# A graph attention layer on one core: signals once per quad, near scores ahead of a group, pieces joined after six quads

## The chip, the cores and the metric

The kernel runs on one core of a Trainium2 chip. The metric is the device time of one execution in microseconds, as the median of the runs.

## The reference

A graph attention layer with 8 heads, its residual, and then a mixture of eight experts, of which each node uses two. This is its core, shortened:

```python
h = (x @ W).reshape(N, H, C)                         # N = 3125, H = 8, C = 256
a_src = einsum('nhc,hc->nh', h, att_src); a_dst = einsum('nhc,hc->nh', h, att_dst)
e = leaky_relu(a_src[src] + a_dst[dst], 0.2)         # 50,000 edges, sorted by dst
m = segment_max(e, dst, N); e = exp(e - m[dst])
denom = segment_sum(e, dst, N)
alpha = e / (denom[dst] + EPS)
out = segment_sum(h[src] * alpha[:, :, None], dst, N)
gnn = out.mean(axis=1) + bias

x = x + gnn(layernorm(x)); x = x + moe(layernorm(x)) # 8 experts of 256 x 256, the best 2
```

Because the mean over heads comes behind the sum over edges, the weights W can be multiplied in after the sum: the kernel adds up the source rows of normalized x, weighted by alpha, per node and head.

## The kernel before, in words

A start (to about 190 us) normalizes x, multiplies it into the scores of sources and targets, and sorts out where blocks of edges end. The **group phase** (to 718 us) is what the change touches. A projection by W, the routing of nodes to experts and the experts follow, to the end of the span.

The 50,000 edges, sorted by target, are 392 blocks of 128. A quad is 4 blocks (QUAD). The blocks form nine groups: seven whole ones of 48 blocks (12 quads; WHOLE is 7), then 32 and 24. A block's edges go to at most 20 neighbouring nodes. Nodes are collected in 100 homes of 32 nodes and what runs over behind them, in an accumulator on the chip with room for three homes at a time (ACC_RING).

Every engine has its own program; they meet at semaphores:

- **POOL** gathers the source rows of each block by an indirect DMA (L780) into a ring of 96 slots, two groups. From group 2 on, ahead of each quad's four gathers, it waits until `block_done` says that the quad two groups before, whose slots it refills, is multiplied.
- **PE** multiplies in `group()`. For each quad it waits for the spread alphas (`spread_ready`), for room in the accumulator (`acc_free`, at the first block and again at the third), and makes two products a block in L1078 (four PE rows a block in the trace, eight columns of heads by 20 nodes wide). Each block's last product adds 1 to `block_done` (L1156 and L1157). The first quad of a group waits for `rescaled` too.
- Between its quads PE does small steps of the **next** group's softmax (`softmax_step`), at quad counts that stand in the call: near scores (L1087, 12 products, `near_done`) behind quad 1; turning the scores (L1094) behind 3; the pieces' gathering (L1099, `pieces_done`) behind 7; the factors' return (L1104, L1105) behind 9; the alphas' turning (L1111, `alphaT_done`) behind 11. Group 7 has (1, 6, 8, 8), the last group none. Behind the last quad comes the branch to the next group, the read of a table `far` and of two words of places; a group whose blocks lie far apart would take another branch, which isn't run on these inputs.
- **DVE** does the softmax: it joins the pieces (L1837), divides, makes the hot matrix of targets (L1773), weighs (L1862 to L1870), waits for `alphaT_done`, makes spreads 0 and 1 (L1900, one per quad, a ring of 8, each waiting for `block_done` of the quad whose place it takes), rescales the accumulator's open homes (L1887, behind all blocks of the group before), makes near hots of the next group (L1617), spreads 2 to 7, the next group's scores (L1760 to L1800, behind `near_done`) and local softmax (to L1824), and spreads 8 to 11.
- **ACT** empties a home when `block_done` has reached its last block: two copies out (L1368), two clearings (L1372, L1374), the last of which gives `acc_free`.
- **SP** loads a group's near scores when `near_done` has freed their place.

## Time and profile before

| | before |
|---|---|
| median of 3 runs | 1076.33 us (1064.79 to 1094.18) |
| the profiled execution | 1063.4 us |
| its span | 1061.7 us, 16352 instructions |
| mean granted clock of TensorE | 0.802 |
| busy: PE, DVE, POOL, ACT | 734.2, 635.8, 566.9, 362.8 us |
| gathers, L780 | 392, 379.4 us of POOL busy |
| products of blocks, L1078 | 1568 rows, 313.7 us of PE busy |

The span is one execution as the profiler recorded it. The group phase is read by the turned alphas, L1111: a group's products run from its own alphas to the next group's, since those are turned behind its eleventh quad. A wait in the trace is put down to the semaphore that came last; where the profile doesn't know the releaser it says "remote". "issue" is time in which an engine waited for nothing that the profile shows.

### The profile page before, as it was taken

The numbers are of one execution on the slowest core, as the hardware profiler recorded it, in microseconds if no ns is written. First come the engines' busy times: TensorE is split into PE (matmuls) and PEld (weight loads), VectorE is DVE, ScalarE is ACT, GpSimd is POOL, SyncE is SP. The second block draws the span as 40 slices with busy tenths as digits, with TensorE's granted clock in tenths as the row PEclk, the third lists the DMA queues.
The fourth block names the chain that finished last, engine by engine and source line by source line (L and its number), as shares of the span: only waits on it lengthen the run. The fifth ranks groups of instructions, "written<-read, shape, count | busy, mean of one in ns | idle before, by whom it ended". The sixth has DMA issues, their size and how long they took to land.

```text
span 1061.7 us, 16352 instructions
## 1 busy us (share of the span) xinstructions
PE 734.2 (69%) x3876; PEld 655.2 (62%) x3877; DVE 635.8 (60%) x1829; ACT 362.8 (34%) x795; POOL 566.9 (53%) x613
## 2 busy tenths in 40 slices
PE   4765320566664765656766647779999998659995
PEld 4764220456654755546556647778888887548884
DVE  6705448564672854646646738665778778654653
ACT  4201110256454433423221112002524441737663
POOL 2172757566666667666666661013322551567686
PEclk9556555587967868877767879989999999889998
DMA  9643334477766856757455443619998865367663
GB/s 313 172 109 81 104 94 127 147 227 238 250 224 193 236 185 199 224 159 203 145 153 157 141 130 102 220 38 348 347 365 304 315 243 163 87 157 118 106 96 40
DMA packets 102473, 192.59 MB, mean 181 GB/s; under 512 B 22875, under 2 KB 61070, under 8 KB 101728
## 3 DMA queue, kind: packets, MB, share of 16 engines
q0 software_dynamic: 30176, 69.02, 27.1%
q1 hardware_dynamic: 57616, 80.31, 23.4%
q10 hardware_dynamic: 14576, 42.02, 10.1%
q8 instruction: 46, 0.75, 0.3%
q14 instruction: 59, 0.48, 0.2%
HBM read 129.20 MB, written 64.06 MB: 182 GB/s over the span
## 4 chain that ended last, share of the span: by engine, by line
DVE 29%; PE 26%; another core or an unknown queue 16%; issue 15%; DMA 6%; ACT 3%; ACTq 1%; DVEq 1%; POOL 1%; POOLq 1%; PEld 0%; SPq 0%; PEldq 0%
PE banks L1078 10%; PE banks L1226 6%; PE banks L1266 3%; PE banks L1279 3%; DVE arena L1900 3%; DMA out<-ring 2%; DMA ring<-agg_table 2%; PE banks L1087 2%; DVE banks L1505 1%; DVE ring L1526 1%; ACT banks L1372 1%; ACT arena L1368 1%; DVE stats L1564 1%; DMA ring<-in_L_gnn_W 1%
## 5 line engine op out<-in xcount | busy, mean ns | idle before, releaser
L780 POOL DMA_INDIRECT ring<-node_table,idx x392 | 379.4, 968 | 229.4 <-issue 113.9
L1078 PE MATMUL banks<-arena,ring 128*128 128x160 f32 x1568 | 313.7, 364 | 149.0 <-issue 54.7
L1078 PEld LDWEIGHTS banks<-arena,ring 128*128 128x128 f32 x1568 | 283.9, 238 | 173.1 <-issue 172.6
L1368 ACT COPY arena<-banks 128x400 f32<-128x400 f32 x200 | 88.6, 495 | 382.3 <-PE banks L1078 165.3
L1226 PE MATMUL banks<-ring 128*128 128x264 f32 x544 | 123.1, 387 | 0.0
L1226 PEld LDWEIGHTS banks<-ring 128*128 128x128 f32 x544 | 103.0, 190 | 17.4
L924 POOL DMA_INDIRECT out<-ring x56 | 89.7, 1602 | 34.0 <-DVE ring L2217 12.2
L1900 DVE TENSOR_TENSOR arena<-hot,banks 128x640 f32<-128x640 f32 x84 | 63.8, 815 | 55.7 <-remote 34.3
L1266 PEld LDWEIGHTS banks<-ring 128*128 128x128 f32 x448 | 59.7, 200 | 26.9 <-issue 19.7
L1266 PE MATMUL banks<-ring 128*128 128x128 f32 x448 | 64.0, 288 | 17.7 <-issue 16.3
L1279 PE MATMUL banks<-arena,ring 128*128 x224 | 60.9, 396 | 5.2 <-ACT ring L1422 4.4
L1226 PE MATMUL banks<-ring,arena 128*128 128x264 f32 x256 | 58.4, 387 | 0.0
L2217 DVE SCALAR_TENSOR_TENSOR ring<-banks,job_w,ring 128x256 f32<-128x256 f32 x56 | 27.1, 483 | 47.0 <-PE banks L1279 26.7
L1372 ACT COPY banks<-zeros 128x400 f32<-128x400 f32 x100 | 50.7, 507 | 9.7 <-issue 4.6
L1226 PEld LDWEIGHTS banks<-ring,arena 128*128 128x128 f32 x256 | 48.5, 190 | 8.2
L1374 ACT COPY banks<-zeros 128x400 f32<-128x400 f32 x100 | 50.0, 500 | 0.0
L910 POOL DMA_INDIRECT slot_table<-arena,slots x42 | 42.1, 1002 | 12.7 <-issue 11.3
L1388 ACT COPY ring<-ring 128x448 f32<-128x448 f32 x30 | 29.0, 1013 | 52.3 <-DMA ring<-agg_table 37.1
L906 POOL COPY arena<-tags 128x3 f32<-128x3 f32 x21 | 3.9, 188 | 80.3 <-DVEq L2073 79.3
L1279 PEld LDWEIGHTS banks<-arena,ring 128*128 128x128 f32 x224 | 39.7, 198 | 10.2 <-issue 6.6
L1422 ACT ACTIVATE ring<-banks,b_sb 128x128 f32<-128x128 f32 x112 | 35.1, 364 | 16.6 <-issue 13.7
L891 POOL TENSOR_TENSOR ring<-ring,bias_bc 128x256 f32<-128x256 f32 x25 | 19.0, 791 | 35.7 <-DMA ring<-in_x 35.7
(421 smaller groups left out, 1022.9 us busy)
## 6 DMA issues: line engine op xcount, KB each, us to landing
agg_table<-arena ACTq DMA_DIRECT2D x100, 400.0 KB
ring<-agg_table SPq DMA_DIRECT2D x25, 1600.0 KB
ring<-slot_table SPq DMA_DIRECT2D x56, 130.0 KB
ring<-node_table,idx POOLq DMA_INDIRECT x392
near_hot<-dst_table SPq DMA_DIRECT2D x28, 192.0 KB
ring<-in_x SPq DMA_DIRECT2D x8, 640.0 KB, 11.8
ring<-in_L_gnn_W SPq DMA_DIRECT2D x4, 1024.0 KB, 9.2
arena<-in_L_ffn_w SPq DMA_DIRECT2D x16, 256.0 KB
```

The source lines that it names most:

```text
L780: pool.indirect_dma_start(rows[:, slot_of(b), :], None, node_table, bass.IndirectOffsetOnAxis(idx[:, b:b + 1], 0)).then_inc(got[got_of(g)] ...
L910: pool.indirect_dma_start(slot_table, bass.IndirectOffsetOnAxis(slots[:, k, t:t + 1], 0), tn[t % TN_RING], None).then_inc(sent[t % TN_RING ...
L924: pool.indirect_dma_start(out, bass.IndirectOffsetOnAxis(xs[j % XS_RING][:, D:D + 1].bitcast(I32), 0), ybuf[j % Y_RING], None, bounds_chec ...
L1078: m = pe.matmul(columns[:, k, bass.ds(at * (UNIT * H), SPREAD * H)], lhs[:, k * P:(k + 1) * P], weights, start=False, stop=True, skip_grou ...
L1226: m = pe.matmul(bank[proj_bank(t)][:, 0:CN], aggt[t % AGG_RING][:, k * H + h, :], W_sb[:, k, h, :], start=(k == 0 and h == 0), stop=(k == ...
L1266: m = pe.matmul(h_bank[j % 2][:, f * P:(f + 1) * P], w1_now[j % 2][:, k, f * P:(f + 1) * P], xsT[j % 2][:, k, :], start=(k == 0), stop=(k ...
L1279: m = pe.matmul(y_bank[j % 2][:, 0:D], h_sb[j % 2][:, f, :], w2_sb[:, bass.ds(e, 1), f, :].rearrange("p e n -> p (e n)"), start=(f == 0), ...
L1368: act.copy(stage[j][:, k * SLOTS * H:(k + 1) * SLOTS * H], views[k]).then_inc(drained, 1)
L1372: act.copy(views[0], zeros[:, 0:1].to_broadcast([P, SLOTS * H]))
L1374: act.copy(views[1], zeros[:, 0:1].to_broadcast([P, SLOTS * H])).then_inc(acc_free, 1)
L1422: g = act.activation(h_sb[j % 2][:, f, :], h_bank[j % 2][:, f * P:(f + 1) * P], ACT.Gelu, bias=b1_sb[:, bass.ds(e, 1), f:f + 1].rearrange( ...
L1900: dve.tensor_tensor(spread[:, s:s + QUAD, :].rearrange("p s (d h) -> p s d h", h=H), hot[:, q * QUAD:(q + 1) * QUAD, :].unsqueeze(3).to_br ...
```

## The change

PE's signal per block becomes one per quad: the quad's last product adds 4 to `block_done`. The near scores of the next group are made at the head of a group's code, ahead of the table's read and the branch, which is behind the last product of the group before; on DVE the near hots that they need move from behind the rescale to behind the weighing, ahead of the wait for the alphas. And pieces are gathered after quad 6 instead of 7.

```diff
-            def group(g, quad, slot, ring, size, nxt, steps, near_at=1, ahead_of_far=0):
+            def group(g, quad, slot, ring, size, nxt, steps, near_ahead=True, ahead_of_far=0):
                 def softmax_step(done):
-                    if turn and done == near_at:
-                        near_scores(g + 1, quad + size // QUAD, kb_of(nxt), chunks_of(nxt))
                     if done == turn:
                         turn_scores(g + 1, kb_of(nxt))
...
+                if near_ahead:
+                    near_scores(g + 1, quad + size // QUAD, kb_of(nxt), chunks_of(nxt))
                 is_far = pe.value_load(far[0:1, bass.ds(g, 1)], min_val=0, max_val=2 * NS)
...
-                            add_block(at, rows[:, (slot + q * QUAD + s) % ROOM, :], spread[:, (ring + q) % SPREAD_RING * QUAD + s, :])\
-                                .then_inc(block_done, 1)
+                            m = add_block(at, rows[:, (slot + q * QUAD + s) % ROOM, :], spread[:, (ring + q) % SPREAD_RING * QUAD + s, :])
+                        m.then_inc(block_done, QUAD)
                         softmax_step(q + 1)
...
-                    group(2 * pair + j, pair * (2 * per_group) + j * per_group, slot_of(j * GB), j * per_group % SPREAD_RING, GB, 0, (3, 7, 9, 11), ahead_of_far=7)
+                    group(2 * pair + j, pair * (2 * per_group) + j * per_group, slot_of(j * GB), j * per_group % SPREAD_RING, GB, 0, (3, 6, 9, 11), ahead_of_far=6)
...
-                      steps_of.get(g, (3, 7, 9, 11)), near_at.get(g, 1), ahead_of_far.get(g, 7))
+                      steps_of.get(g, (3, 6, 9, 11)), g < WHOLE, ahead_of_far.get(g, 6))
...
                 weigh(g)
+                if g < GROUPS - 3:
+                    near_hots(g + 1)
                 dve.wait_ge(alphaT_done, g + 1)
...
                     rescale(g, *bounds[g])
-                    if g < GROUPS - 3:
-                        near_hots(g + 1)
                     spreads(g, 2, SPREAD_RING)
```

PE's program at the head of the loop over groups, here behind the alphas' turning of the first group. The ISA rows of L1087 load the weights of its products; `near_hot` is what near scores multiply by. Before:

```order
L1111 MATMUL banks<-ident,arena 128x16x8 x2
L1200 UNCONDITIONAL_BRANCH
L1200 ISA
L1132 TENSOR_LOAD far
L1132 ISA x2
L1133 COMPARE_AND_BRANCH
...
L1147 REGISTER_ALU [waits rescaled]
L1150 REGISTER_ALU [waits spread_ready]
...
L1083 REGISTER_ALU
L1087 ISA [waits near_hot_ready]
L1087 MATMUL banks<-arena,near_hot 128x32
```

And of the change:

```order
L1111 MATMUL banks<-ident,arena 128x16x8 x2
L1200 UNCONDITIONAL_BRANCH
L1200 ISA
L1087 ISA [waits near_hot_ready]
L1087 MATMUL banks<-arena,near_hot 128x32
...
L1132 TENSOR_LOAD far
L1132 ISA x2
L1133 COMPARE_AND_BRANCH
...
L1147 REGISTER_ALU [waits rescaled]
L1150 REGISTER_ALU [waits spread_ready]
```

The twelve products of L1087 stood behind the first quad's eight and now stand ahead of the table's read; the wait for `near_hot_ready` stands ahead of the wait for `rescaled`.

DVE's program at the boundary between the first group and the second, from the last step of the weighing on; `banks` at L1887 is the accumulator. Before:

```order
L1870 TENSOR_TENSOR arena<-banks,arena 128x384 [waits dve_chain]
L1900 TENSOR_TENSOR arena<-hot,banks 128x640 [waits block_done,alphaT_done]
L1891 COPY arena<-banks 128x384
L1900 TENSOR_TENSOR arena<-hot,banks 128x640 [waits block_done]
L1883 REGISTER_ALU [waits block_done]
L1887 ISA [waits acc_free]
...
L1617 TENSOR_TENSOR near_hot<-near_hot,near_key 128x1536 [waits dve_chain,in_near]
L1900 TENSOR_TENSOR arena<-hot,banks 128x640 [waits block_done] x6
```

And of the change, where lines stand one lower:

```order
L1869 TENSOR_TENSOR arena<-banks,arena 128x384 [waits dve_chain]
L1616 TENSOR_TENSOR near_hot<-near_hot,near_key 128x1536 [waits in_near]
L1899 TENSOR_TENSOR arena<-hot,banks 128x640 [waits block_done,alphaT_done]
L1890 COPY arena<-banks 128x384
L1899 TENSOR_TENSOR arena<-hot,banks 128x640 [waits block_done]
L1882 REGISTER_ALU [waits block_done]
L1886 ISA [waits acc_free]
...
L1899 TENSOR_TENSOR arena<-hot,banks 128x640 [waits dve_chain,block_done]
L1899 TENSOR_TENSOR arena<-hot,banks 128x640 [waits block_done] x5
```

The near hots moved past two spreads, the rescale and their waits for `alphaT_done` and `block_done`; what they wait for themselves (`in_near`, the load) is as before.

## Rows read from the trace of the kernel before

**Rows 1.** The page's first line: span of the profiled execution, instructions.

```profile
span 1061.7 us, 16352 instructions
```

**Rows 2.** Windows: start:end, us, busy of PE, PEld, DVE, ACT, POOL (instructions); clock, DMA, GB/s.

```profile
190.80:264.70 73.90, 48.89 (x212) 43.22 (x213) 39.63 (x86) 36.81 (x86) 44.53 (x47) 0.68 0.66 209
...
399.80:470.10 70.30, 43.65 (x230) 39.01 (x229) 39.39 (x87) 24.76 (x58) 48.03 (x49) 0.78 0.63 197
...
612.20:665.40 53.20, 34.03 (x220) 32.49 (x221) 30.11 (x78) 8.77 (x21) 20.69 (x22) 0.84 0.38 114
```

**Rows 3.** The gathers' line, 204 to 646 us; what ended POOL's idle time before them.

```profile
L780 POOL DMA_INDIRECT ring<-node_table,idx x296: 940/946/2258, 204.5 to 642.7; - x148
...
  issue: 77.7, 255
  PE banks L1078: 40.9, 22
  remote: 38.7, 19
```

**Rows 4.** Timeline, POOL: start us, us, engine, line, operation [idle before <-releaser].

```profile
396.56 0.94 POOL L780 DMA_INDIRECT ring<-node_table,idx  x1 [2.02 <-PE banks L1078]
...
408.35 0.95 POOL L780 DMA_INDIRECT ring<-node_table,idx  x1 [2.10 <-remote]
```

**Rows 5.** Timeline around a late signal, group 2, columns as in rows 4.

```profile
370.82 0.26 DVE L1820 TENSOR_TENSOR piece_in<-chunk_sel,ends 128x96 f32<-128x96 f32 x1
...
375.21 0.33 PE L1099 MATMUL banks<-piece_in,head_sel 128*8 128x96 f32 x2
...
384.64 0.25 DVE L1837 COPY piece_all<-banks 8x96 f32<-8x96 f32 x1 [9.25 <-remote]
384.83 0.89 ACT L1368 COPY arena<-banks 128x400 f32<-128x400 f32 x2 [4.74 <-remote]
384.83 0.94 POOL L780 DMA_INDIRECT ring<-node_table,idx  x1 [1.80 <-remote]
```

**Rows 6.** Timeline: scores at the start, and near scores of group 4.

```profile
59.66 9.53 PE L1002 MATMUL banks<-va,ring 128*128 128x8 f32 x44
...
88.77 0.37 DVE L1544 TENSOR_TENSOR score_all<-banks,rstd 128x200 f32<-128x200 f32 x1 [40.00 <-remote]
...
416.30 3.01 PE L1087 MATMUL banks<-arena,near_hot 128*128 x24
...
426.01 0.56 DVE L1798 TENSOR_TENSOR edge_e<-ring,banks 128x384 f32<-128x384 f32 x1 [4.88 <-remote]
```

**Rows 7.** Timeline: the boundary from group 2 to group 3.

```profile
399.75 0.49 PE L1111 MATMUL banks<-ident,arena 128*128 128x128 f32 x3
...
408.16 0.82 DVE L1900 TENSOR_TENSOR arena<-hot,banks 128x640 f32<-128x640 f32 x1 [8.71 <-remote]
...
411.72 1.76 DVE L1617 TENSOR_TENSOR near_hot<-near_hot,near_key 128x1536 f32<-128x1536 int32 x1 [0.51 <-DVE banks L1887]
...
411.88 4.63 PE L1078 MATMUL banks<-arena,ring 128*128 128x160 f32 x16 [8.81 <-DVEq L1888]
```

**Rows 8.** Waits, 190 to 705 us: line <- releaser: us in total, times, longest.

```profile
PE banks L1078 <- ACT banks L1374: 42.2, 17, 5.9
...
DVE piece_all L1837 <- remote: 32.9, 5, 9.2
...
DVE piece_all L1837 <- issue: 7.8, 1, 7.8
...
DVE edge_e L1798 <- remote: 6.1, 2, 4.9
...
DVE edge_e L1798 <- PE banks L1087: 5.2, 2, 3.4
```

**Rows 9.** Timeline: ACT drains one home.

```profile
378.39 0.89 ACT L1368 COPY arena<-banks 128x400 f32<-128x400 f32 x2 [4.69 <-PE banks L1078]
...
379.58 0.51 ACT L1374 COPY banks<-zeros 128x400 f32<-128x400 f32 x1
```

More of the change, by code:

```diff
@@ L1155, in group @@
                                 skip_runtime_bounds_check_because="a byte of places is 32 * (home % 3) + less than 16")
-                            add_block(at, rows[:, (slot + q * QUAD + s) % ROOM, :], spread[:, (ring + q) % SPREAD_RING * QUAD + s, :])\
-                                .then_inc(block_done, 1)
+                            m = add_block(at, rows[:, (slot + q * QUAD + s) % ROOM, :], spread[:, (ring + q) % SPREAD_RING * QUAD + s, :])
+                        m.then_inc(block_done, QUAD)
                         softmax_step(q + 1)
                 with pe.Else():
-                    far_steps = sorted({n for n in (*steps, near_at) if turn and n})
+                    far_steps = sorted({n for n in steps if turn})
                     for done in far_steps:
@@ L1201, in _ @@
                 for j in range(2):
-                    group(2 * pair + j, pair * (2 * per_group) + j * per_group, slot_of(j * GB), j * per_group % SPREAD_RING, GB, 0, (3, 7, 9, 11), ahead_of_far=7)
+                    group(2 * pair + j, pair * (2 * per_group) + j * per_group, slot_of(j * GB), j * per_group % SPREAD_RING, GB, 0, (3, 6, 9, 11), ahead_of_far=6)
             steps_of = {WHOLE: (1, 6, 8, 8), GROUPS - 1: (0, 0, 0, 0)}
-            near_at = {WHOLE: None}
             ahead_of_far = {WHOLE: 1, GROUPS - 1: 0}
```

## The prediction

> **What bounds the kernel now.** The span is 1061.7 us [rows 1]; the profiled execution took 1063.4 us, 12.9 below the runs' median of 1076.33, so a sum made on the profile is moved up by 12.9 for the median. The change touches the group phase alone, and I read first which engine paces it, by the engines' busy time in single groups. From one group's turned alphas to the next's take 73.90 us in the first group and 70.30 in the fourth; PE is busy 48.89 and 43.65 of that, DVE 39.63 and 39.39, POOL 44.53 and 48.03 [rows 2]. No engine is full. Group 6, during which the gathers end, takes 53.20 us for the same 48 blocks.
>
> So the next view is the line that issues the gathers. From 204.5 to 642.7 us it issues 296: 438.2 / 296 = 1.48 us each, 71 per 48 [rows 3]. Without a stop one costs 0.946 us and 77.7 / 255 = 0.305 us to issue: 1.25, or 60.0 per 48. The rest is 40.9 + 38.7 = 79.6 us in 41 stops, in all of which POOL waits for a quad of two groups before ("remote" is a wait whose releaser the profile doesn't name; it ends by the same signal) [rows 3]. Two such stops stand 11.79 us apart, 396.56 to 408.35 [rows 4], and that is eight gathers (8 x 1.25 = 10.0) and a stop of about 1.8. Six of these are 70.7 us, a group's time. **POOL's cycle of eight gathers and one wait for PE's signal is the period**, and 41 x 0.305 of the stops would be issue anyway: 79.6 - 12.5 = 67 us, or 1.64 a stop, is all that earlier signals can give while gathers last.
>
> Why does the signal come so late? In the timeline PE gathers the pieces at 375.21 and is done within 0.33 us; DVE takes them at 384.64 after 9.25 us of idleness, and ACT and POOL, which wait for other things, are released at 384.83, 0.2 us later [rows 5]. PE's signals thus arrive in bursts, and the burst falls where POOL stands and its transfers run dry. There are two readings: late because there are many signals, one per block, or late because the products queued ahead of them are done later than their records say. For the first speaks that the small steps with a single signal are late only behind blocks. Against it speaks the start of the program: 44 products of the score line end at 59.66 + 9.53 = 69.19 with one signal, and DVE, which stands 40.00 us for it, is released at 88.77, 19.6 us later, with no block signal yet sent [rows 6]. I go by the second at about three to one.
>
> **The change, part by part.** (a) *392 signals become 98.* Every quad's last product still signals, and POOL waits for whole quads, so no gather can be released by an earlier block than before. By the second reading the saving is 0. By the first, lateness shrinks up to fourfold; the bounds are 0 and the 67 us of POOL's stops. I take 0, the nearer to the start's one late signal.
>
> Here the Trainium skill speaks for a gain: "TensorE: Matmul & The Clock Gate", section "The cost: per-tile semaphore tail", gives each increment about 26.3 ns of serial tail and calls a single one on the last product sound. By it, as an estimate, 294 increments fewer would be 7.7 us of PE. No row here shows that tail.
>
> (b) *Near scores before the first quad.* Before, PE makes them behind the first quad: in group 3 at 416.30, 3.01 us of products, and DVE takes them at 426.01 after 4.88 us of waiting [rows 6]. Now they stand behind the last quad of the group before. There PE stands 8.81 us anyway until the first product of group 3 at 411.88, because DVE, though the alphas were turned at 399.75 + 0.49 = 400.24, got them at 408.16 and rescales first [rows 7]. The 3.0 us fit in it with 5.8 to spare, where the table read and the branch, which come behind them now, have to lie too. Without that cover they would cost the 3.0 us that they take, 21 in the seven groups in which they are moved. On DVE the 1.76 us of near hots [rows 7] move from behind the rescale to ahead of the alphas' wait, which lasts 8.71 us [rows 7]: hidden. Where DVE has no such wait, the same 1.76 us are before the first spreads instead of behind them, and PE's first quad is later by that. The wait for near scores (6.1 + 5.2 = 11.3 us in four waits [rows 8]) goes: about 11.3 / 6 = 2, with the 1.76 some 3 us a group off the softmax chain on DVE.
>
> (c) *Pieces joined a quad sooner.* DVE stood for the pieces 32.9 + 7.8 = 40.7 us in six waits [rows 8]. A quad is 70.7 / 12 = 5.9 us, so the join moves up by at most 5.9 where DVE's input to it is ready. It nearly is: in group 2 DVE had it at 370.82 + 0.26 = 371.08, 4.1 us before PE came to it [rows 5], and (b) makes it 3 earlier, 7.1 against the 5.9 needed. Where it isn't ready, PE would stand, with its products and so POOL's signal behind it, for the remainder, at most the 5.9. What is late next is the burst: the join ends when PE's signal arrives, and this moves in whole cycles of POOL.
>
> (b) and (c) together make the chain from flags to alphas up to 9 us shorter per group. But the chain isn't what paces a group: POOL is. How much of the 9 us reaches POOL no row says: 0 if its cycle doesn't notice, 6 x 9 = 54 if all of it does. I choose one stop less per group, 6 x 1.64 = 10 us, near the lower end, since POOL's stops in the middle of a group, as at 396.56 [rows 4], lie far from what the chain delivers. Behind the last gather the chain does count: there a quad is 53.20 / 12 = 4.4 us [rows 2], and with the 1.76 of near hots that is 6 us, once (group 7 keeps its steps).
>
> (d) *ACT drains later.* ACT waited for the block with which a home ends; now it hears of the quad's last. Of the 100 homes only 24 end on a quad's last block (counted from the sorted edges), so 76 are handed over one to three blocks later. A drain takes 378.39 to 380.09, 1.70 us [rows 9], and three homes of room lie ahead of PE. PE stood for ACT's clearing 42.2 us in 17 waits [rows 8]. With bursts as above, a block's own signal came with its quad's anyway, so I take 0. Without that cover it is up to three blocks, 3 x 5.9 / 4 = 4.4 us, per wait.
>
> Sum: 0 - 10 - 6 + 0 = -16. From 1063.4 that is 1047; on the runs' median 1076.3 - 16 = **1060 us**, 1.5% faster.
>
> **The rivals.**
> *The signals were the delay.* For: the bursts release three engines at once [rows 5]. Against: the start [rows 6]. POOL's stops then shrink to half or to their floor, -34 to -67, and with the tail's 6: 1036 to 1003; I put it at 1015, chance 0.19.
>
> *The chain paces more than I think.* Where DVE stands 8 to 9 us for pieces and alphas at a boundary [rows 5, 7], spreads come late and PE with them; the change would then give PE some quads of lead, half the 54 and the tail: -30, 1046. Chance 0.13.
>
> *A signal costs PE's own time.* Four blocks' 16 product records take 4.63 us with their four signals [rows 7], 1.16 us a block; if a tenth of that were the signal's, 294 fewer would be 34 us of PE. PE bounds only once the gathers are over, with some 80 blocks left (32 and 24 of the last two groups, and the end of group 6's 48): 60 signals fewer, 7 us, 1076.3 - 16 - 7 = 1053. Against it: PE stands idle a third of every group [rows 2], so elsewhere it wins nothing. Chance 0.03. The Trainium skill's tail (same page and section) is the rule for this rival.
>
> *ACT's drains come late and PE stands for them.* This is the case that ends slower. In groups 0 and 1 some 21 homes end per group (counted from the edges), 1.75 a quad, each 1.70 us of ACT [rows 9], so ACT's work for a quad is 3.0 of its 5.9 us. If the quad's first home, which it could start some two blocks sooner, now begins with the second, PE's first products of the next quads wait for room. At 1 us a quad over the 24 quads of these two groups that is +24: 1100. It decides from about 0.7 us a quad on (24 x 0.7 = 17 eats the 16). For it: the 42.2 us that PE already stands there [rows 8]. Against it: the lateness of every signal. Chance 0.17.
>
> *Nothing comes of it.* POOL's cycle doesn't notice, the tail is off the end: 1076, within the "same" below.
>
> **How the numbers follow.** Forecast and "nothing" together 0.48: 0.30 for about 1060, 0.18 for about 1076. Signals 0.19, chain 0.13, a signal's own cost 0.03, ACT 0.17. The runs of before lie between 1064.79 and 1094.18, so about 2% (1055 to 1098 as limits) is what a measurement can tell from no change. Faster by more: signals, chain and the signal's own cost, 0.35. Slower: 0.17. The range goes from 1014, which leaves out the signals' far half (0.09), to 1097, which leaves out most of ACT's case (0.10). The likeliest case's own range is 1045 to 1076: the 10 us of stops may be 0 or 20, and the tail 0 to 6.
>
> **What would show it.** (a) right: POOL's stops still near 1.6 us beyond issue, 30 to 41 of them between the same gathers, and DVE's release after the start's scores as late as 88.8; wrong: most stops gone, gathers at 1.3 us each. (b): near scores end before the first quad, and DVE's wait for them is gone; wrong if PE's idle time at the boundary grows beyond 8.8 us. (c): pieces on DVE a cycle earlier and no PE wait for its input above 2 us. (d): PE's wait for ACT's clearing stays near 42 us; at 60 and more the slower rival holds. A time below 1040 makes the reading of the lateness wrong, one above 1090 that of ACT or of the boundary.

## The result, and the profile after

In the first measurement the changed kernel took 1089.66 us (median of 4 runs, 1084.04 to 1102.49) and before took 1077.28 (4 runs, 1064.79 to 1094.18). The ratio of these medians is 1.0115; the ratio on record is 1.0226, 95% interval 1.0181 to 1.0272: slower, where 1.5% faster was forecast, though the interval doesn't settle whether by more than 2%. The runs of both kernels fall into clusters, and the ratio on record leaves out what lies over 1.5% above a kernel's fastest run and so hangs on where that one run fell (for e1 below it gives 1.0118, 1.0051 to 1.0186, where the medians over all runs stand at 0.998), so that below I give medians and differences of means over all runs instead (one run of before of 3647.81 us apart).

The profiled execution of the changed kernel is a late one, 39.1 us longer than that of before [rows 1]. The page's first line and its row of the products (busy us, mean ns | idle before, what ended most of it):

```profile
span 1100.8 us, 16330 instructions
...
L1078 PE MATMUL banks<-arena,ring 128*128 128x160 f32 x1568 | 313.7, 366 | 128.6 <-ACT banks L1373 70.1
```

PE is busy with blocks as long as before, 313.7 us. The times of L1111 in the timeline tell where the 39 us are. The first group's alphas are turned at 229.85 us, in before at 190.84 (190.80 is where the first stretch of [rows 2] begins): 39 us late already. Group 7's are turned at 703.8 and 665.4: still 38 us. **The whole difference of these two profiles lies ahead of the groups**, in a stretch whose code the change does not touch. The timeline of the changed kernel there (start us, us, engine, line, operation [idle before <-releaser]):

```profile
146.16 5.16 PE L1087 MATMUL banks<-arena,near_hot 128*128 128x32 f32 x24
...
202.07 0.55 DVE L1797 TENSOR_TENSOR edge_e<-ring,banks 128x384 f32<-128x384 f32 x1 [35.47 <-remote]
...
229.85 0.90 PE L1111 MATMUL banks<-ident,arena 128*128 128x128 f32 x3 [5.18 <-DVE arena L1869]
...
231.65 5.32 PE L1087 MATMUL banks<-arena,near_hot 128*128 x24 [0.90 <-DVE near_hot L1616]
...
236.78 5.26 PE L1078 MATMUL banks<-arena,ring 128*128 128x160 f32 x24
...
241.23 0.94 POOL L780 DMA_INDIRECT ring<-node_table,idx  x1 [43.13 <-PE banks L1078]
```

And of before:

```profile
149.65 5.16 PE L1087 MATMUL banks<-arena,near_hot 128*128 128x32 f32 x24
...
153.58 0.94 POOL L780 DMA_INDIRECT ring<-node_table,idx  x1 [7.55 <-issue]
...
157.62 0.56 DVE L1798 TENSOR_TENSOR edge_e<-ring,banks 128x384 f32<-128x384 f32 x1
```

The near scores of group 0 were made by 146.16 + 5.16 = 151.3 us, and DVE took them at 202.07, 50.7 us later, when POOL had made its last gather of the first two groups (197.2). In before the same products ended at 154.8, behind a stop of POOL of 7.55 us, and DVE took them at 157.62 without having waited; the changed kernel's POOL stopped there too, but for 4.40 us alone (to 153.07). Everything behind hangs on the 97th gather, the first that needs a quad finished: 241.23 here, 204.52 in before, and the span ends 860 and 857 us behind it.

The groups themselves, with what answers to [rows 2], [rows 3] and [rows 8]. Windows (start:end, us, busy of PE, PEld, DVE, ACT, POOL; clock, DMA, GB/s), groups 0, 3 and 6:

```profile
229.85:301.30 71.45, 48.45 (x212) 44.34 (x213) 40.96 (x87) 34.75 (x80) 39.24 (x40) 0.69 0.64 203
434.50:508.30 73.80, 46.19 (x230) 42.54 (x229) 40.07 (x87) 26.11 (x60) 47.77 (x50) 0.75 0.60 181
647.20:703.80 56.60, 42.21 (x222) 38.18 (x221) 29.88 (x78) 10.31 (x24) 22.41 (x24) 0.76 0.36 112
```

The gathers' line, and what ended POOL's idle time before them:

```profile
L780 POOL DMA_INDIRECT ring<-node_table,idx x296: 940/946/2422, 241.2 to 679.8; - x148
...
  issue: 79.3, 260
  PE banks L1078: 73.7, 14
  remote: 41.4, 22
```

296 gathers in 679.8 - 241.2 = 438.6 us, in before in 438.2 [rows 3]. Without the one stop of 43.13 POOL stands 72.0 us in 35 stops; before, without its first of 4.47, 75.1 in 40. **POOL's stops, and with them the time of the groups together, are what they were in these two profiles.** The waits (line <- releaser: us in total, times, longest) show that inside the group much has moved all the same:

```profile
PE banks L1078 <- ACT banks L1373: 70.1, 24, 6.2
...
DVE edge_e L1797 <- remote: 38.3, 3, 35.5
...
PE banks L1078 <- DVEq L1887: 9.7, 4, 6.2
...
DVE piece_all L1836 <- remote: 3.8, 3, 1.3
```

and of before the row that [rows 8] leaves out:

```profile
PE banks L1078 <- DVEq L1888: 45.9, 6, 13.5
```

DVE's wait for the pieces fell from 40.7 us to 6, and PE's wait for DVE's rescale at the boundaries from 45.9 to 9.7. PE's wait for ACT's clearing rose from 42.2 to 70.1. At the boundary into group 3, the place of [rows 7], the near scores stand where the idle 8.81 us were:

```profile
434.51 0.49 PE L1111 MATMUL banks<-ident,arena 128*128 128x128 f32 x3
...
438.39 0.82 DVE L1899 TENSOR_TENSOR arena<-hot,banks 128x640 f32<-128x640 f32 x1 [5.83 <-remote]
...
440.37 4.63 PE L1078 MATMUL banks<-arena,ring 128*128 128x160 f32 x16 [5.37 <-ACT banks L1373]
...
444.80 2.94 PE L1087 MATMUL banks<-arena,near_hot 128*128 x24
...
448.44 0.74 PE L1078 MATMUL banks<-arena,ring 128*128 128x160 f32 x2 [0.70 <-issue]
```

The boundary costs PE 0.70 us now, as the change meant, but 8 us earlier it stood 5.37 for ACT.

### The profile page after: what moved, and what is told of

Read it like the earlier page. It is cut to its first block, busy times and chain, and to the rows that moved or that the text cites. A ratio compares the mean times of both kernels' runs of the same rounds, so it can differ in the third digit from the quotient of the medians.

```text
span 1100.8 us, 16330 instructions
## 1 busy us (share of the span) xinstructions
PE 747.9 (68%) x3876; PEld 673.0 (61%) x3877; DVE 635.2 (58%) x1829; ACT 363.6 (33%) x795; POOL 563.2 (51%) x613
## 4 chain that ended last, share of the span: by engine, by line
PE 29%; DVE 20%; issue 16%; another core or an unknown queue 15%; DMA 7%; ACT 4%; POOL 3%; ACTq 2%; POOLq 2%; DVEq 1%; PEld 0%; SPq 0%; PEldq 0%
PE banks L1225 10%; PE banks L1078 8%; DMA out<-ring 5%; PE banks L1002 4%; DVE arena L1899 3%; POOL ring L780 2%; ACT banks L1371 2%; ACT arena L1367 1%; PE banks L1265 1%; PE banks L1278 1%; DVE banks L1504 1%; PE banks L1050 1%; DMA ring<-in_x 1%; ACTq L1353 1%
## 5 line engine op out<-in xcount | busy, mean ns | idle before, releaser
L780 POOL DMA_INDIRECT ring<-node_table,idx x392 | 379.4, 968 | 263.0 <-issue 112.4
L1078 PE MATMUL banks<-arena,ring 128*128 128x160 f32 x1568 | 313.7, 366 | 128.6 <-ACT banks L1373 70.1
L1078 PEld LDWEIGHTS banks<-arena,ring 128*128 128x128 f32 x1568 | 288.3, 241 | 149.7 <-issue 149.0
L1371 ACT COPY banks<-zeros 128x400 f32<-128x400 f32 x100 | 50.7, 507 | 8.5 <-issue 4.5
L1002 PE MATMUL banks<-va,ring 128*128 128x16 f32 (+1 forms) x200 | 40.4, 341 | 17.6 <-issue 17.3
L1002 PEld LDWEIGHTS banks<-va,ring 128*128 128x128 f32 x200 | 41.8, 314 | 16.6 <-issue 16.2
L910 POOL DMA_INDIRECT slot_table<-arena,slots x42 | 41.5, 987 | 12.7 <-issue 11.3
L1278 PEld LDWEIGHTS banks<-arena,ring 128*128 128x128 f32 x224 | 40.1, 200 | 10.8 <-issue 7.1
## 6 DMA issues: line engine op xcount, KB each, us to landing
ring<-in_x SPq DMA_DIRECT2D x8, 640.0 KB, 12.1
```

The lines of the kernel that those rows point to most:

```text
L780: pool.indirect_dma_start(rows[:, slot_of(b), :], None, node_table, bass.IndirectOffsetOnAxis(idx[:, b:b + 1], 0)).then_inc(got[got_of(g)] ...
L910: pool.indirect_dma_start(slot_table, bass.IndirectOffsetOnAxis(slots[:, k, t:t + 1], 0), tn[t % TN_RING], None).then_inc(sent[t % TN_RING ...
L1002: m = pe.matmul(bank[score_bank(a, t)][:, t * n:(t + 1) * n], xT[:, t, k * P:(k + 1) * P], va[:, k, 0:H + NX] if a == 0 else va_of[1][:, k ...
L1078: m = pe.matmul(columns[:, k, bass.ds(at * (UNIT * H), SPREAD * H)], lhs[:, k * P:(k + 1) * P], weights, start=False, stop=True, skip_grou ...
L1278: m = pe.matmul(y_bank[j % 2][:, 0:D], h_sb[j % 2][:, f, :], w2_sb[:, bass.ds(e, 1), f, :].rearrange("p e n -> p (e n)"), start=(f == 0), ...
L1371: act.copy(views[0], zeros[:, 0:1].to_broadcast([P, SLOTS * H]))
```

## The experiments

**Theories.** S: the loss is ahead of the groups, where PE's signals wait behind gathers for a time that varies, and the change has little part in it. A: one signal per quad makes ACT drain later. N: near scores and pieces stand in the wrong place.

Each series ran before beside its kernels, on one chip. The table has every run that gave a time: medians in us, and the difference of the means to before of the same series with its 95% half-width (1.96 standard errors, which is too narrow for rows of 4 to 6 runs: the first row's would be 18.6 by Student's t). "Early start" and "held" are explained below.

| kernel | runs | median | before, runs | difference |
|---|---|---|---|---|
| the change, first measurement | 4 | 1089.7 | 1077.3, 4 | +13.1 +- 14.5 |
| e1, the change again | 12 | 1080.2 | 1082.7, 23 | +1.3 +- 7.4 |
| e2, the change, signals per block | 6 | 1079.1 | same | +0.4 +- 9.2 |
| e3, before, signals per quad | 6 | 1080.3 | same | +0.2 +- 10.5 |
| e4, before, near scores ahead | 12 | 1071.9 | same | -4.0 +- 7.6 |
| e5, before, held | 12 | 1072.2 | 1075.5, 35 | -5.1 +- 4.2 |
| e6, the change, held | 12 | 1075.2 | same | -1.7 +- 4.0 |
| e7, as e6, groups 0 and 2 behind | 12 | 1074.6 | same | -3.6 +- 3.4 |
| e8, as e6, signals per block | 12 | 1072.9 | same | -4.4 +- 3.3 |
| e9, the change a third time | 6 | 1082.2 | 1080.0, 17 | -2.6 +- 8.8 |
| e10, before, narrow gathers | 8 | 1078.9 | same | -3.7 +- 8.0 |
| e11, before, early start | 6 | 1060.8 | same | -18.6 +- 7.1 |
| e12, the change, early start | 12 | 1071.2 | 1078.4, 23 | -6.5 +- 6.1 |
| e13, before, early start | 12 | 1062.3 | same | -13.9 +- 5.7 |
| e14, as e12, groups 0 and 2 behind | 12 | 1067.7 | 1079.8, 24 | -11.7 +- 5.0 |
| e15, as e12, signals per block | 6 | 1063.6 | same | -11.9 +- 8.4 |
| e16, the change, early start | 12 | 1066.4 | same | -12.1 +- 5.2 |
| e17, before, early start | 6 | 1061.1 | same | -16.9 +- 5.6 |
| e18, before, early start, signals per quad | 12 | 1067.4 | 1079.5, 17 | -15.6 +- 4.9 |

### The change again, and its parts alone (e1 to e4, e9)

e1 and e9 are the changed kernel itself. e2 undoes its first part, e3 makes that part alone, and e4 the second part alone:

```diff
-                            add_block(...).then_inc(block_done, 1)
+                            m = add_block(...)
+                        m.then_inc(block_done, QUAD)
```

> The changed kernel itself, once more, for a second profile. In its first profile the whole difference to before lies ahead of the groups: first alphas turned at 229.85 us instead of 190.84, because the near scores' signal of group 0 reached DVE 50 us late, and from there to the turned alphas of group 7 it took 473.9 us against 474.5. Theory S (the start): the start is late by a varying amount from run to run, so this profile has first alphas somewhere between 190 and 230 us and 474 us of groups behind it. Theory A (ACT): the drains start later, so PE's wait for ACT's clearing is again at 60 us or more (70 in the first profile, 42 before), and the groups take longer than 474 us wherever the start is on time, by about 20 us. Theory N: the loss is in the order of near scores and pieces, and this shows as PE standing at the boundaries.

> The change without its first part: a signal per block again, near scores ahead and pieces after six quads. Theory A: PE's wait for ACT falls back to about 42 us and the time to the kernel's before or below it, 1060 to 1077. Theory S: as slow as the change where the start is late, whatever the signals; the time lies with the change at about 1088. Theory N: as slow as the change, with the loss at the boundaries.

> The kernel before with the first part alone: one signal of 4 per quad. Theory A: slower than before by about the whole 2%, 1088 to 1100, and PE's wait for ACT at 60 us and more. Theory S: no difference to before except through the start, 1065 to 1090 with the groups at 474 us. Theory N: as before, 1077. If the number of signals were what makes them late, this one would be faster than before by 30 us or more.

> The kernel before with the second part alone: near scores ahead of a group's first quad, near hots ahead of the wait for the alphas. Theory N: slower than before by most of the 2%, 1085 to 1095, with PE's first products of a group later behind the turned alphas than the 11.6 us of before. Theory A: as before or up to 10 us faster, 1066 to 1077. Theory S: no difference other than by the start.

> The changed kernel a third time, beside more runs of before, to see how much of the 2.26% is a matter of which runs were drawn. Theory S: both kernels have the same two or three clusters of times, set by how late the near scores' signal of group 0 is, and the change adds some 4 us ahead of the first product: medians within 1% of each other, the ratio between 0.995 and 1.012. Theory A or N, a steady cost in the groups: again 1.015 to 1.025.

e1's profile is as late as the first one: near scores made by 146.0, their signal at 202.1, the 97th gather at 241.0, the end 859 us behind it. e9's is on time: 150.5, 151.4, 206.2, and 860. In e2 the signal was 18.6 us late and the 97th gather at 222.4. Over all profiles of this study the 97th gather goes between 199.8 and 241.2 us, and the end is 854 to 873 us behind it, with no order by kernel. The three series together have 22 runs of the changed kernel and 44 of before: medians 1082.6 and 1080.8, difference of the means +2.2 +- 5.4 us. The 2.26% of the first four runs did not come back. e3 and e4 lie under what A and N had wanted of them (1088 to 1100 and 1085 to 1095), and e3 isn't the 30 us faster that it would be if the number of signals made them late. Beyond that the parts alone can't be told from before in these runs: the spread of one kernel, some 40 us, hides whatever they do. That speaks for S and says how much has to be taken out before A and N can be judged.

### The start held (e5 to e8)

One wait more on POOL, ahead of the last 36 gathers of group 1, in before (e5) and in the changed kernel (e6). e7 makes near scores of groups 0 and 2 behind the first quad again (and group 0's near hots behind the rescale), e8 signals per block.

```diff
             first_far_scores()
+            pool.wait_ge(near_done, 1)
             gather(1, AHEAD_OF_TABLES, GB)
```

> The kernel before, with one wait added on POOL: ahead of the last 36 gathers of group 1 it waits until DVE could take the near scores of group 0, so that this signal no longer stands behind gathers. Theory S (the start decides): in six profiles so far the first refilling gather (the 97th) went between 204.5 and 241.2 us and the span ended 857 to 865 us behind it, whatever the kernel; the signal came 0 to 56 us late. With the wait it comes within 5 us, the 97th goes at 203 to 210 us in every run, and the times gather at 1060 to 1070 us, without the 1077 to 1093 us that 18 of 23 runs of before showed. If the lateness is not from gathers, the spread of the runs stays, and the wait costs 5 to 50 us.

> The changed kernel with the same wait on POOL. Theory S: the spread goes here too, and what is left against the other kernel with the wait is the change's own effect. From the profiles: near scores ahead of the first group cost 4 us there (6.0 us from the turned alphas to the first product instead of 2.3), from the 97th gather to the last is 2 to 4 us shorter (434 to 436 against 438), the tail behind it 1 to 3 us longer: within 5 us of the other kernel, 1064 to 1072. Theory A (ACT's drains): 15 to 25 us slower than the other kernel with the wait.

> As the changed kernel with the wait on POOL, but near scores in groups 0 and 2 are made behind the first quad, and group 0's near hots behind the rescale, as before the change. If the 4 us ahead of group 0's first product are what the change loses where the start is on time, this is 3 to 6 us faster than the one with all near scores ahead, and first products come 2 to 3 us behind the turned alphas. If not, the same.

> The changed kernel with the wait on POOL, and a signal per block again. Theory A, that one signal per quad makes ACT late: faster than with one per quad by 5 to 20 us, and PE's wait for ACT falls from 60 or more to about 42 us. Theory S: the same within 4 us; signals neither cost nor bring anything, since POOL's cycle of eight gathers holds the groups.

The timeline of e5 shows what a gather does to the signal and what the end of the gathers does:

```profile
135.73 5.17 PE L1088 MATMUL banks<-arena,near_hot 128*128 128x32 f32 x24
...
148.16 0.95 POOL L780 DMA_INDIRECT ring<-node_table,idx  x1 [0.30 <-issue]
...
153.04 0.56 DVE L1799 TENSOR_TENSOR edge_e<-ring,banks 128x384 f32<-128x384 f32 x1 [8.45 <-remote]
153.17 0.94 POOL L780 DMA_INDIRECT ring<-node_table,idx  x1 [4.07 <-remote]
```

The scores were made by 140.9, the signal came 4 us after POOL's last gather was issued, at 149.1, to DVE and POOL at once. The spread went from 37 us (before, 35 runs, 1066.62 to 1103.74) to 18 in e5, 13 in e6 and 9 in e7 and e8, and none of these 48 runs is above 1084.1; of before 8 of 35 are. So S holds for the upper part of the spread; the median of before fell by 3 us only, and the expected 1060 to 1070 was too low. The change is 3.4 +- 3.9 us slower than the other held kernel, e8 0.7 +- 3.2, e7 1.5 +- 3.3: small, and not placed.

### What holds the gathers (e10)

```diff
-                    pool.indirect_dma_start(rows[:, slot_of(b), :], None, node_table,
+                    to, table = (rows[:, slot_of(b), :], node_table) if g < 2 else (rows[:, slot_of(b), 0:H], score_table)
+                    pool.indirect_dma_start(to, None, table,
```

> The kernel before, where from group 2 on each gather brings 8 numbers a row (32 bytes) from the table of scores instead of 264; the other columns keep what the ring held, so the sums are of old rows. As many gathers, as many rows, the same waits, 1/33 of the bytes. What it tells: why PE's signals come late and what paces a group. If it is the bytes in flight, signals come within 1 us, POOL's stops go, and a group takes POOL's 60 us or less. If it is the number of rows or POOL's issuing, the stops and the 71 us per 48 gathers stay as they are.

```profile
L781 POOL DMA_INDIRECT ring<-score_table,idx x295: 940/947/2284, 204.2 to 642.1; - x148
...
  issue: 77.1, 253
  remote: 40.8, 23
  PE banks L1079: 36.4, 19
```

The same stops, 77.2 us in 42, the same 438 us, with 1/33 of the bytes. (The trace has 295 of the 296 gathers; the start of this kernel gathers whole rows as before.) So it isn't the volume of data that makes PE's signals late in the groups or a group 71 us long; what is left is the gathers' number, their 128 rows each, or their issuing, and no run here tells these apart.

### The second scores first (e11 to e13, e16, e17)

At the start DVE waits for a signal that stands alone [rows 6]. POOL now makes 8 gathers and then waits for that signal itself (with e5's wait further on):

```diff
-            gather(0, 0, AHEAD_OF_VECTORS)
-            pool.wait_ge(va_summed, 2)
-            gather(0, AHEAD_OF_VECTORS, AHEAD_OF_STRETCHES)
+            gather(0, 0, 8)
+            pool.wait_ge(score_done, 3)
+            gather(0, 8, 17)
...
```

> The kernel before with POOL's start put otherwise: after 8 gathers it waits for the second scores' signal of PE, then makes 9 more, the stretches and the rest, and ahead of the last 36 gathers of group 1 it waits for the near scores' signal. If PE's signals are late behind gathers, also one that stands alone, DVE takes the second scores at 70 to 74 us instead of 88.8, the first alphas are turned 10 to 16 us sooner, at 175 to 182, and the time falls by 5 to 14 us, to where POOL's own 96 gathers allow. If the lateness at the start has another cause, DVE takes them near 88 and POOL's wait costs what it lasts, 10 us or more.

> The changed kernel with the start put as in e11_start_scores_first, beside that kernel. With the early start PE is ready for its first product some 15 us before POOL has finished its first 96 gathers, so the 4 to 11 us that near scores ahead of group 0 cost are hidden there. Theory S: nothing is left of the change: within 4 us of the other, both near 1060. Theory A or N, a steady cost in the groups: 8 us and more slower than the other.

> The kernel of e11_start_scores_first once more, as what the changed one with the same start is held against on the same chip: 1056 to 1065 us, and 1.0 to 2.0% faster than before.

> The changed kernel with the early start again (the kernel of e12_change_scores_first), beside the two that undo a part and the one that undoes all: 5 to 9 us slower than the one that undoes all.

> The kernel before with the early start again (that of e13_before_scores_first), against which the other three are held: 1056 to 1065 us in the median.

Timeline of e11:

```profile
47.18 21.50 PE L1003 MATMUL banks<-va,ring 128*128 128x8 f32 x100 [0.27 <-DVE va L1539]
...
68.72 0.36 DVE L1545 TENSOR_TENSOR score_all<-banks,rstd 128x200 f32<-128x200 f32 x1 [20.47 <-PE banks L1003]
...
68.95 0.94 POOL L780 DMA_INDIRECT ring<-node_table,idx  x1 [10.46 <-PE banks L1003]
```

The products end at 47.18 + 21.50 = 68.68, as in before at 69.19 [rows 6]. Without gathers behind them DVE has the signal 0.04 us later, with them it had it 19.6 us later. **That shows the cause of the lateness: gathers in flight, and one signal is enough to be late.** Over the three series the kernel before with this start takes 1061.9 us (median of 24 runs, none above 1074.5) against 1079.1 for before without it (143 runs of all series, 29% of them above 1085): 16.5 +- 2.6 us faster in the mean, the best version of this study. That is the worth of both waits together, since e11 has e5's too.

With most of the start's variation gone the change can be judged: 24 runs each, 1067.9 against 1061.9, difference of the means **+6.1 +- 3.1 us, 0.6%** (+7.4 +- 4.6 in e12 and e13, +4.8 +- 4.3 in e16 and e17). S, which wanted nothing left, falls for this part; the 8 us and more of A or N are above the mean, though inside its interval. The start isn't pinned altogether: in e13's profile the near scores' signal came before POOL had to wait for it, the gathers went on without a stop to 194.2, and the first alphas were turned at 205.65, where the other six profiles of e11 to e17 have 178.5 to 182.3.

### Which part costs the 6 us (e14, e15, e18)

e14 is the changed kernel with the early start and the near scores of groups 0 and 2 behind the first quad (and group 0's near hots behind the rescale), e15 that with signals per block, e18 before with the early start and signals per quad alone.

> The changed kernel with the early start, but near scores of groups 0 and 2 behind the first quad and group 0's near hots behind the rescale. On one chip the changed kernel with the early start was 7.4 us (plus or minus 4.6) slower than before with it, and its first product came 13.2 us behind the turned alphas against 2.1. If these 11 us ahead of the first product are the cost, this kernel is 4 to 9 us faster than the changed one with the early start, and its first product is 2 to 3 us behind the alphas. If the cost is in the groups behind, the same within 3.

> The changed kernel with the early start and a signal per block again. If one signal per quad costs (ACT hears of a home's end up to three blocks late; PE's wait for ACT 62 to 71 us instead of 41 to 53), this is 4 to 9 us faster than the changed one with the early start. If PE's wait for ACT only takes the place of other waits, the same within 3.

> The kernel before with the early start and the first part of the change alone, one signal of 4 per quad. Over three chips the early start took 1061.9 us (median of 24 runs) without the change and 1067.9 (24 runs) with it. If one signal per quad costs these 6 us (ACT's drains later, PE's wait for ACT at 60 us and more), this kernel lies at 1066 to 1070, 1.0% under before. If not, at 1060 to 1064, 1.6% under before, and the cost is in the order of near scores or pieces.

The first group in e12, where gathers are in flight when its alphas are turned:

```profile
180.55 0.90 PE L1112 MATMUL banks<-ident,arena 128*128 128x128 f32 x3 [6.55 <-DVE arena L1870]
...
182.25 5.32 PE L1088 MATMUL banks<-arena,near_hot 128*128 x24 [0.80 <-issue]
...
194.70 0.89 PE L1079 MATMUL banks<-arena,ring 128*128 128x160 f32 x2 [7.13 <-remote]
...
205.34 0.94 POOL L780 DMA_INDIRECT ring<-node_table,idx  x1 [7.42 <-PE banks L1079]
```

and in e14:

```profile
179.85 0.90 PE L1112 MATMUL banks<-ident,arena 128*128 128x128 f32 x3 [4.95 <-DVE arena L1872]
182.83 2.50 PE L1079 MATMUL banks<-arena,ring 128*128 128x160 f32 x8 [2.08 <-issue]
```

Near scores ahead put 13.2 us between the turned alphas (181.45) and the first product; behind, 2.1. But in e14 the 97th gather goes at 203.3, only 2 us sooner than in e12, and the kernel is only 1.6 +- 3.3 us faster than the changed one (e12 and e16 together; against e16 of its own series it is 0.4 +- 3.5 slower). Most of the 11 us are hidden behind POOL, which is not done with its first 96 gathers before 197.

For the signals, PE's wait for ACT in e16 (signals per quad) and in e17 (per block):

```profile
PE banks L1079 <- ACT banks L1374: 60.8, 19, 5.9
```

```profile
PE banks L1079 <- ACT banks L1375: 51.9, 19, 5.8
```

Over the ten profiles with signals per block it is 40.0 to 52.8 us, mean 46.6, over the ten with one per quad 52.1 to 75.1, mean 64.2. The two groups differ in more than the signal, and the order of near scores matters: with near scores ahead the wait goes from a mean of 45.4 us (e2, e4, e8, e15) to 66.5 (the eight profiles of the change, e7 and e14 among them), with them behind the first quad as in before from 47.5 (six profiles) to 55.0 (e3 and e18). So the signal per quad makes PE stand longer for ACT, some 8 us by itself and some 21 together with near scores ahead.

What of it reaches the end isn't settled. e18 is 4.1 +- 3.2 us slower than before with the early start in the other series, but as far under the before of its own series (-15.6) as those were under theirs (-13.9 to -18.6), and its profile makes the second scores 7 us later than those of e12 to e17, ahead of anything that was changed; e15 has four runs at 1059 to 1064 and two at 1078 to 1079, and tells nothing. Nor do the profiles show a loss in the groups: from the 97th gather to the end of the span it is 859.5 us in the mean of six profiles with the groups of before (before, e5, e10, e11, e13, e17) and 859.4 in six of the change (the first, e1, e6, e9, e12, e16), a difference of -0.1 +- 5.0. **Where the 6 us are lost stays open.** The Trainium skill's tail of 26.3 ns an increment ("TensorE: Matmul & The Clock Gate", "The cost: per-tile semaphore tail") would spare PE in e18, as an estimate, 7.7 us; no run here shows such a gain, and 4.1 +- 3.2 points the other way.

## Why the prediction was wrong

**The forecast's sign** was wrong: 16 us faster stood against 13.1 slower in the first four runs; over all runs without an added wait it is +2.2 +- 5.4, with the start held +3.4 +- 3.9, with the early start +6.1 +- 3.1. No set of runs shows the gain; "nothing comes of it", chance 0.18, is nearest. Two steps failed: the gain of (b) and (c), 16 us of which none was measured, and the start, a term that was put at nothing.

**(b) and (c) together** is where the 16 us were lost: "I choose one stop less per group, 6 x 1.64 = 10 us" measured 1.6 us in the first profile: 72.0 us in 35 stops less 35 x 0.305 is 61.3, before 75.1 in 40 gives 62.9. Over the six profiles of each named above the 296 gathers take 437.3 us with the change and 438.1 without, 0.9 +- 2.1 less. The shorter chain did reach PE, 36 us less standing at the boundaries, but PE then stood 28 us longer for ACT, and POOL's gathers took as long as before. The 6 us behind the last gather didn't come either: from it to the last product it is 75.0 us in before and 76.3 in the changed kernel, 77.4 and 77.9 over the six of each.

**What I did not price at all** is the start. I took the profiled span of before, 12.9 us under its median, as the kernel's own time, and moved the sum up by 12.9 as if that were the same in both kernels. But the start varies from run to run: the 97th gather went 37 us later in the first profile of the change than in that of before, and with POOL waiting for two signals before fell to a median of 1061.9, with none of 24 runs above 1074.5. Late signals behind gathers are the largest varying term that the profiles show, up to 56 us for the near scores of group 0. Since the first difference did not come back in e1 and e9, most of it was this and not the change; four runs of each were too few, and +13.1 +- 14.5 holds zero.

**What bounds the kernel.** That POOL's gathers and its stops pace the groups held in every profile (eight gathers are the commonest stretch between two stops, 22 of 38 in before; 4 and 12 occur as well). That the number of signals is not what makes them late was right: with 98 signals instead of 392 POOL stands as long [rows 3 and the row of L780 above], and the start, which I had taken for the deciding row [rows 6], decided it when tried (e11).

**(a)** 0 was right for the lateness.

**(b)** The step "the 3.0 us fit in it with 5.8 to spare" held at the boundary into group 3 and failed at the first group, for which I had not read the row: there PE has no such idle time, and the first product moved from 2.1 to 6.0 us behind the turned alphas, or to 13 where gathers were in flight. DVE's waits went as said: the one for the pieces from 40.7 to 6 us, that for near scores inside the groups from 11.3 to 2.8 (38.3 without the first of 35.5).

**(d)** "I take 0" may be the step that had the sign, but that is argued and not shown. PE's wait for ACT rose by 28 us in the first profile, over the 60 that I had named for the slower rival, while that rival's +24 is far above the 6 us that were seen in all. "With bursts as above, a block's own signal came with its quad's anyway" is therefore false for part of the homes. The wait took the place of others in good part: the groups of the profiles are no longer for it.

**The range** of 1014 to 1097 holds 1089.66, but mostly because it was wide for the other side. One rival's sum is off: half the 54 and the tail's 6 are 33, not 30, so that it should have stood at 1043.

## What to carry to other kernels

When runs of one kernel spread by more than the effect looked for, find first what the spread is in the trace and pin it; here one wait of POOL for another engine cut it from 37 to 18 us, and with a second one further ahead before ran 16 us faster. A shorter chain is worth what the pacing engine loses by it, so price it there, and ask of each signal made rarer which waiter wanted the early one. A step that idle time covers at one boundary has to be looked up at the first one too, where there may be none.

## What the runs showed of the hardware

Signals. A signal of PE that stands alone came 0.04 us after its products where POOL had stopped its gathers (the second scores of e11, and the same in e12 to e18), and mostly 11 to 56 us after them where gathers were in flight (the second scores, the near scores of group 0). At the near scores of group 0 POOL stops, without an added wait, in seven of the eight profiles of such kernels, and the length of that stop goes with the lateness: at most 1.6 us late with stops of 5.7 us and more (before, e3, e4, e9, e10), 18.6 and 50.6 us late with stops of 4.9 (e2) and 4.4 (the first profile of the change), 56 without a stop (e1). Why the stop varies no run tells. The late signal came 4 us after POOL's last gather had been issued in e5 and in the first profile, 8 in e1, and in e2 while gathers went on. In the groups, gathers of 32 bytes a row delayed as much as gathers of 1056 (e10).

Products. In before, e2, e4 and e10 the records of the second scores' products are as dense with gathers as without, 21.50 us for 100 in before and e11, and only the signal is late. In the other eight profiles without the early start the products themselves are. From the first profile of the change:

```profile
53.59 16.17 PE L1002 MATMUL banks<-va,ring 128*128 128x8 f32 x75 [0.27 <-DVE va L1537]
...
76.65 0.17 PE L1002 MATMUL banks<-va,ring 128*128 128x8 f32 x1 [2.44 <-issue]
78.74 0.17 PE L1002 MATMUL banks<-va,ring 128*128 128x8 f32 x1 [1.92 <-issue]
...
89.24 2.95 PE L1002 MATMUL banks<-va,ring 128*128 128x8 f32 x14 [0.53 <-issue]
```

Until 69.8 us one product follows another every 0.21 us; then they come singly or in twos, up to 2.8 us apart, while PE waits for nothing that the profile shows; and behind POOL's last gather (84.7) they are dense again. DVE had this signal at 92.23, 0.04 us after the last product.

Another engine. DVE's instructions thin out in the same way. Two of them in before, where gathers go out from 100.6 to 146.0 without a stop, and the same two in e5, where POOL had stopped from 121.1 to 124.4:

```profile
138.69 0.57 DVE L1713 COPY ring<-banks 128x392 f32<-128x392 f32 x1 [0.83 <-DVE ring L1712]
140.09 0.42 DVE L1714 TENSOR_SCALAR ring<-ring,node_ids 128x392 f32<-128x392 f32 x1 [0.83 <-DVE ring L1713]
```

```profile
131.41 0.57 DVE L1714 COPY ring<-banks 128x392 f32<-128x392 f32 x1
132.01 0.42 DVE L1715 TENSOR_SCALAR ring<-ring,node_ids 128x392 f32<-128x392 f32 x1
```

They start 1.40 us apart in before and 0.60 in e5, and the chain from L1707 to L1720 (one line lower in e5) takes 15.6 and 6.5 us. In e13's late start DVE's softmax of group 0 goes at 0.7 to 1.4 us an instruction from 168 to 202 us, under gathers without a stop. So gathers in flight went with delays in more than PE's signals; what they hold back in an engine, and whether the recording of the profile has a part in it, no run tells.
